# Seven block products for the four gate and up products of the second feed-forward part, in two passes of 1024 tokens

## The reference, cut to what matters

```python
Wg, Wu, Wd = dequant_nvfp4(gate...), dequant_nvfp4(up...), dequant_nvfp4(down...)
gate = jnp.einsum('th,nh->tn', xt, Wg)      # 2048 x 512 times 512 x 4096
up = jnp.einsum('th,nh->tn', xt, Wu)
gelu = jnp.tanh(0.7978845608028654 * (gate + 0.044715 * gate ** 3)) * gate * 0.5 + gate * 0.5
out = jnp.einsum('tn,hn->th', gelu * up, Wd)
...
g = _silu(out)
x = x + s * g                               # s: the recurrence over 1024 steps of each sequence
```

## Time and profile before

| | |
|---|---|
| median of 3 runs (lowest to highest) | 3084.49 us (3082.95 to 3084.57) |
| the profiled execution: its own time | 3083.76 us |
| span from first to last instruction | 3082.0 us |
| PE busy | 3028.1 us, 98% of the span |
| DVE busy | 1843.8 us, 60% |
| ACT busy | 1585.5 us, 51% |
| POOL busy | 1408.2 us, 46% |
| granted TensorE clock, mean | 0.995 |

### The profile page before, as it was taken

How to read it: one execution, slowest core, us unless ns; L and a number is a source line. 1 busy time by engine, 2 the same in 40 slices (tenths; PEclk the granted TensorE clock), 3 DMA queues, 4 the chain that set the end, 5 groups by cost and what they waited for, 6 DMA issues and landing times. The chain is left out here.

```text
span 3082.0 us, 61209 instructions
## 1 busy us (share of the span) xinstructions
PE 3028.1 (98%) x23896; PEld 2508.2 (81%) x23896; DVE 1843.8 (60%) x3306; ACT 1585.5 (51%) x3891; POOL 1408.2 (46%) x2351
## 2 busy tenths in 40 slices
PE   8999989999999999999999899999999999999999
PEld 7888867888888888888888678788888888888887
DVE  6112167788877887877888533625555555444545
ACT  5221358787788787878787633443333332112112
POOL 2322336666667666666676444323332232222212
PEclk9999999999999999999999999999999999999999
DMA  3100121111111111111111155311011110000004
GB/s 94 31 21 28 57 69 35 54 55 55 43 49 50 56 56 56 50 49 46 56 53 50 49 193 150 101 31 31 28 39 38 37 31 28 21 25 24 28 14 164
DMA packets 130240, 165.67 MB, mean 54 GB/s; under 512 B 9936, under 2 KB 72144, under 8 KB 129920
## 3 DMA queue, kind: packets, MB, share of 16 engines
q1 hardware_dynamic: 120592, 144.49, 15.6%
q10 hardware_dynamic: 9296, 17.04, 1.5%
q0 software_dynamic: 64, 0.23, 0.0%
HBM read 127.91 MB, written 33.82 MB: 52 GB/s over the span
## 5 line engine op out<-in xcount | busy, mean ns | idle before, releaser
L1489 DVE SCALAR_TENSOR_TENSOR b_zt<-b_rx,b_cw,b_zt 128x512 f32<-128x512 f32 x576 | 472.7, 821 | 22.0 <-POOL b_rx L1698 3.2
L70 PE MATMUL bank<-b_XH,b_wh 128*128 128x512 f32 x1024 | 456.5, 446 | 9.1 <-ACT b_zt L1238 7.6
L72 PE MATMUL bank<-b_XH,b_wl 128*128 128x512 f32 x1024 | 403.0, 394 | 0.0
L71 PE MATMUL bank<-b_XL,b_wh 128*128 128x512 f32 x1024 | 402.6, 393 | 0.0
L70 PE MATMUL bank<-b_XH,b_qh 128*128 128x512 f32 x1024 | 398.7, 389 | 0.0
L72 PE MATMUL bank<-b_XH,b_ql 128*128 128x512 f32 x1024 | 398.4, 389 | 0.0
L71 PE MATMUL bank<-b_XL,b_qh 128*128 128x512 f32 x1024 | 398.4, 389 | 0.0
L2758 POOL TENSOR_TENSOR b_QHL<-b_qhd,b_QHH 128x512 fp32r<-128x512 f32 x124 | 176.5, 1427 | 474.8 <-ACT b_QHH L2530 472.3
L2530 ACT CAST b_QHH<-b_qhd 128x512 fp32r<-128x512 f32 x124 | 76.8, 622 | 415.2 <-PE bank L72 254.1
L2659 DVE TENSOR_TENSOR b_QACC<-b_QACC,bank 128x512 f32<-128x512 f32 x232 | 159.0, 687 | 148.5 <-PE bank L72 148.3
L2652 DVE TENSOR_TENSOR b_qhd<-b_g,bank 128x512 f32<-128x512 f32 x128 | 87.5, 684 | 267.1 <-PE bank L72 160.9
(11 more groups left out here) (268 smaller groups left out, 7505.9 us busy)
## 6 DMA issues: line engine op xcount, KB each, us to landing
b_abc<-tmp_a SPq DMA_DIRECT2D x64, 256.0 KB, 3.4
b_gbc<-tmp_g SPq DMA_DIRECT2D x64, 256.0 KB, 3.9
tmp_og<-b_gg SPq DMA_DIRECT2D x64, 256.0 KB, 2.4
b_mo<-tmp_og SPq DMA_DIRECT2D x64, 256.0 KB, 3.2
b_wr<-in_Wk SPq DMA_DIRECT2D x16, 256.0 KB, 3.2
b_wr<-in_Wq SPq DMA_DIRECT2D x16, 256.0 KB, 4.3
b_wr<-in_Wv SPq DMA_DIRECT2D x16, 256.0 KB, 2.7
b_wr<-in_Wg SPq DMA_DIRECT2D x16, 256.0 KB, 4.2
```

The lines of the kernel that those rows point to most:

```text
L70: e.do.matmul(out, wh, xh, start=first and k == 0, stop=False)
L71: e.do.matmul(out, wh, xl, start=False, stop=False)
L72: m = e.do.matmul(out, wl, xh, start=False, stop=last and k == n - 1)
L1489: e.do.scalar_tensor_tensor(out=z[:, :], in0=rx[:, j:j + 512], scalar=cw[:, u // 2, KIND[name[0]], j:j + 1], in1=z[:, :], op0=ALU.mult, op ...
```

## The change

**Seven products.** The gate and up rows of a hidden slice (128 + 128), the two halves of the 512 inputs and two groups of 512 tokens form a 2 x 2 times 2 x 2 block product. Eight block products (6 matmuls each, 48 in all) become seven (42): m1 to m7, from the blocks a11, a12 (gate) and a22 and the sums s1 to s4 of weight blocks, and the blocks b11, b21, b22 and the sums t1 to t4 of input blocks. The weight sums are made by DVE for every block (weight_sums, 4 additions of 128 x 512). The input sums are made once for each pass.

**Two passes.** 1024 tokens a pass, 32 steps g each, 64 in all. A pass goes over all 16 blocks j, two steps for each (the hidden slices of 128). The weights are unpacked in the first pass only; each float32 tile (wG, wU, wD) is also stored to DRAM (weight_kept) and loaded again in the second pass (weight_again), where its sums, high parts and low parts are made again. Unpacking takes five integer operations for a tile rather than six.

**Sums in PSUM.** ACT copies m1 from its bank into a second one (seed); m6, m7 and m4 are added there by mm3_onto, and m2 onto m1's own bank and m3 onto m5's bank. In between ACT copies m5 and the second sum to SBUF (fifth, second_sum), DVE adds m7's state (third_sum), forms the second gate (gate1) and multiplies twice (hidden0, hidden1), ACT applies gelu twice. m4 of step g, issued in step g + 1, waits for third_sum of step g.

**Order on PE in a step:** m1; m4 and m3 of the step before; fill; m5, m6; fill; m2; fill; m7; fill. A fill is one down product (6 matmuls), and in eight of the steps also a rate product. There are three banks for the fills.

**Other.** XH1 and XL1 hold 1024 tokens; the input blocks of the second pass are kept in DRAM and swapped in during steps 31 and 32 (next_block_high, next_block_low). The first output rows are written after the first pass. All output DMAs are issued by SP.

The diff, cut to its core:

```diff
@@ in ffn1_pe @@
-        mm3(e, kb[:, :], [(t["qh"][s][:, par, q * 256 + s2 * 128:q * 256 + s2 * 128 + 128],
-                           t["ql"][s][:, par, q * 256 + s2 * 128:q * 256 + s2 * 128 + 128],
-                           XH[:, 2 * q + par, cols(n)], XL[:, 2 * q + par, cols(n)])
-                          for q in range(2) for par in range(2)]).then_inc(S["gu1"], 1)
...
+def mm3_onto(e, out, pairs):
+    for wh, wl, xh, xl in pairs:
+        e.do.matmul(out, wh, xh, start=False, stop=False, skip_group_check=True)
+        e.do.matmul(out, wh, xl, start=False, stop=False, skip_group_check=True)
+        m = e.do.matmul(out, wl, xh, start=False, stop=True, skip_group_check=True)
+    return m
...
+WEIGHTS = ("a11", "s1", "s2", "a12", "s3", "a22", "s4")
+PRODUCTS = {"m1": ("a11", "b11"), "m5": ("s1", "t1"), "m6": ("s2", "t2"), "m2": ("a12", "b21"), "m7": ("s3", "t3"),
+            "m4": ("a22", "t4"), "m3": ("s4", "b22")}
+RATE_AT = {4: 0, 10: 1, 16: 2, 22: 3, 40: 4, 46: 5, 52: 6, 58: 7}
@@ in ffn1_pe @@
+    def product(name, g):
...
+            if name == "m4":
+                e.wait_ge("c22", g + 1)
...
+        pairs = [(t["wh"][i][:, r, c], t["wl"][i][:, r, c], hi[:, r, :], lo[:, r, :]) for r in range(2)]
+        (mm3 if name in ("m1", "m5") else mm3_onto)(e, bank[to][:, :], pairs).then_inc(S[name], 1)
...
+    for g in range(2 * STEPS + 4):
+        if g <= LAST:
+            product("m1", g)
+        if 0 < g <= LAST + 1:
+            product("m4", g - 1)
+            product("m3", g - 1)
+        fill(g, 0)
+        if g <= LAST:
+            product("m5", g)
+            product("m6", g)
+        fill(g, 1)
+        if g <= LAST:
+            product("m2", g)
+        fill(g, 2)
+        if g <= LAST:
+            product("m7", g)
+        fill(g, 3)
@@ in ffn1_dve, without the swap of blocks @@
+    for g in range(2 * STEPS + 4):
+        j, odd, live, older = g // 2, g % 2 == 1, g <= LAST, 0 < g <= LAST + 1
+        sums, gate_w, up_w, down_w = odd and j + 1 < STEPS, not odd and j + 2 < 16, not odd and j + 1 < 16, odd and j < 16
+        if g:
+            fill(g - 1, 3)
+        if sums:
+            weight_sums(e, t, j + 1, 0)
+        if gate_w:
+            weight_codes(e, t, "G", j + 2, 0)
+        if older:
+            hidden0(g - 1)
+        if sums:
+            weight_sums(e, t, j + 1, 1)
+        if gate_w:
+            weight_codes(e, t, "G", j + 2, 1)
+        if older:
+            gate1(g - 1)
+        if sums:
+            weight_sums(e, t, j + 1, 2)
+        fill(g, 0)
+        if g - 3 in RATE_AT:
+            scan(RATE_AT[g - 3])
+        if older:
+            hidden1(g - 1)
+        if g - 2 in RATE_AT:
+            reset(RATE_AT[g - 2])
+            enter(RATE_AT[g - 2])
+        if gate_w:
+            weight_scaled(e, t, "G", j + 2)
+        if up_w:
+            weight_codes(e, t, "U", j + 1, 0)
+        if down_w:
+            weight_codes(e, t, "D", j, 0)
+        fill(g, 1)
...
+        fill(g, 2)
+        if up_w:
+            weight_scaled(e, t, "U", j + 1)
+        if down_w:
+            weight_scaled(e, t, "D", j)
+        if live:
+            third_sum(g)
@@ in ffn1_pool, the low parts @@
+    for g in range(2 * STEPS + 4):
...
+        if before:
+            down_low(e, t, j - 1, 0)
+        if following:
+            weight_low(e, t, 0, j + 1)
+        if older:
+            low(g - 1, 0)
+        if before and j < STEPS:
+            weight_low(e, t, 5, j)
+        if following:
+            weight_low(e, t, 1, j + 1)
+        if before and j < STEPS:
+            weight_low(e, t, 6, j)
+        if following:
+            weight_low(e, t, 2, j + 1)
+        if older:
+            low(g - 1, 1)
+        if following:
+            weight_low(e, t, 3, j + 1)
+        if before:
+            down_low(e, t, j - 1, 1)
+        if following:
+            weight_low(e, t, 4, j + 1)
```

More of the change, by code:

```diff
@@ L2099, in mix0_over @@
     e.wait_ge("mxr2", 80)
[L2104 to L2124, removed]
@@ L2127, in q_slot @@
[L2127 to L2155, removed]
@@ L2158, in down_at @@
[L2158 to L2170, removed]
-    for j in range(16):
[L2172 to L2185, removed]
@@ L2188 @@
[L2188 to L2204, removed]
+STEPS = 32
+LAST = 2 * STEPS - 1
+WEIGHTS = ("a11", "s1", "s2", "a12", "s3", "a22", "s4")
+SUMS = {"s1": 1, "s3": 2, "s2": 3, "s4": 4}
@@ L2207, in ffn1_tiles, with fill_banks, down_at @@
+def fill_banks():
+    bank, before, last, n = {}, {}, {}, 0
+    for g in range(2 * STEPS + 4):
+        for place in fills(g):
+            for what in place:
+                b = FILL_RING[n % 3]
+                bank[what], before[what] = b, last.get(b)
+                last[b] = what
+                n += 1
+    return bank, before
+FILL_BANK, FILL_BEFORE = fill_banks()
+def down_at(j, b, o):
+    return 8 * j + 4 * b + o
 def ffn1_tiles(t, at, arena):
     low = at + 32768
-    t.puts("pk", [128, 512], I32, (at, at + 2048))
@@ L2220, in ffn1_tiles @@
[L2220 to L2225, removed]
+    four = (at, at + 2048, low, low + 2048)
@@ L2489, in ffn1_pe, with fill @@
-    for j in range(1, 16):
-        for g in range(8):
-            hidden(j, g)
-            if g == DOWN_AT:
-                for i in range(len(down_order(j - 1))):
-                    down(j - 1, i)
-            if j < 9 and g < 2:
-                rate(j - 1, g)
-    for n in range(4):
-        for o in range(4):
-            down(15, 4 * n + o)
-            if n > 1 and o == 1 or n == 1 and o == 3:
-                for i in range(4):
-                    row(4 * (n - 1) + i)
-    for i in range(4):
-        row(12 + i)
+    def fill(g, place):
+        for what in fills(g)[place]:
+            if what[0] == "down":
+                down(*what[1:])
+            if what[0] == "rate":
+                rate(*what[1:])
+            if what[0] == "row":
+                row(what[1])
+            if what[0] == "sum":
+                sum_rows_pe(e, k, m, what[1], taken(what))
+            if what[0] == "turn":
+                norm_turn_pe(e, k, m, what[1], taken(what))
@@ L2627, in ffn1_act, with gate, fill @@
-    for n in range(4):
-        for o in range(4):
-            gate(n, o)
-        if n:
-            store(n - 1)
-    store(3)
+    def gate(q):
+        p, b = divmod(q, 2)
+        for o in range(4):
+            e.wait_ge("ac", down_at(16 * p + 15, b, o) + 1)
+            e.do.activation(t["QACC"][o][:, cols(b)], t["QACC"][o][:, cols(b)], ACT.Silu).then_inc(S["fsil"], 1)
+    def fill(g, place):
+        for what in fills(g)[place]:
+            if what[0] == "rate":
+                rate(*what[1:])
+            if what[0] == "sum":
+                sum_rows_act(e, k, m, what[1], bank[FILL_BANK[what]])
+                if what[1] % 2:
+                    norm_root_act(e, m, what[1] - 1)
+                    norm_root_act(e, m, what[1])
+            if what[0] == "turn":
+                norm_turn_act(e, k, m, t, what[1], bank[FILL_BANK[what]])
@@ L2654, in add, with third_sum @@
[L2654 to L2659 removed]
+    X, Y, M = t["l1x"], t["l1y"], t["l1m"]
+    def third_sum(g):
+        e.wait_ge("m7", g + 1)
+        e.wait_ge("r5c", g + 1)
+        e.do.tensor_tensor(t["c22"][:, :], t["c22"][:, :], bank[Q_BANK[g % 2]][:, :], ALU.add).then_inc(S["c22"], 1)
@@ new lines, in row, with fill @@
+        x = t["x1f"][i % 8]
+        e.do.tensor_tensor(x[:, :], bank[FILL_BANK["row", i, 0]][:, :], x[:, :], ALU.add).then_inc(S["y"], 1)
+    def fill(g, place):
+        for what in fills(g)[place]:
+            if what[0] == "down":
+                add(*what[1:])
+            if what[0] == "row":
+                row(what[1])
+            if what[0] == "sum" and what[1] % 2:
+                for i in (what[1] - 1, what[1]):
+                    norm_stats_dve(e, m, i)
+                for i in (what[1] - 1, what[1]):
+                    norm_dve(e, m, i)
```

1163 lines of the change are left out of this document (722 added, 441 removed), and 9 rows, old and new, of tables (AGAIN, SEMAPHORES).

## The result

The changed kernel takes 3168.6 us (median of 4 runs, 3165.9 to 3171.5) against 3084.5: 1.0271 times as long, 95% interval 1.0258 to 1.0284. The sign of the forecast held, its size didn't: +13 us became +84, and the time lies 29 us above the top of the range. The profiled span is 3169.8 us.

What follows compares the result with a forecast made beforehand. PE's matmul list bounded the kernel before; DVE was to bound the changed first pass. Terms -87 + 59 + 11 + 21 + 6 + 3 = +13 us gave 3098 us, range 3030 to 3140.

Steps and rivals of the forecast that it cites:

- Step 1: PE, both passes: 64 steps lose one block product of 6 matmuls each, 384 x 0.2264, -87.0 us.
- The lock and its share: First pass: POOL's SBUF operations make DVE's port work wait for 0.58 of their time, 9.7 us a pair of steps.
- Covered: Rival, first pass: waits fall into DVE's idle time, a pair stays under 30.0 us, PE sets the pace; 3012, chance 0.20.
- Step 2: Pairs 1 to 14 of the first pass: DVE needs 34.4 us against PE's 30.0, for 13.5 pairs, +59 us.
- DVE over 95%: Expected sign in first-pass windows: DVE busy over 95%, with PE at about 87%.
- the one in my rivals: Rival, first pass: late DVE delays ACT, pushing POOL's low parts into the unpacking; share 0.75, +98 us, 3137, chance 0.20.
- cover of 2.7 us: PE's one fill and m1 ahead of its wait for third_sum: 2.7 us, used up once, not in every step.
- step 3: Four recurrence slices, first pass: DVE's 4.65 us and 3.5 of waits, against 5.4 of PE's rate products, +11 us.
- Step 4: Start: DVE makes third_sum of step 0 by 1999.5 and of step 1 by 2019, later than PE needs; +21 us.
- Step 5: Step 31: DVE's 17.8 us and 5.2 of waits against 15.0, less the cover, +6 us.
- The second pass "at nothing": Second pass: DVE needs 9.9 + 2.7 of 30.0 us a pair, so PE sets the pace and nothing is added.
- Step 6: Tail: rows 8 to 11 later, last quarter's states loaded late, one queue storing all rows; +3 us (0 to 8).

Runs made afterwards that it cites:

- experiment 1: Changed kernel with POOL's low parts of weights and down weights cut to 32 of 256 columns after the first block: 3087.9 us, 1.0014 times before.
- experiment 4: Changed kernel with DVE making third_sum before the two scale multiplications of the tile in hand, same operations otherwise: 3133.7 us, 1.0160 times before.
- experiment 5: Changed kernel with POOL's two recurrence operations (`enter`) cut to 128 of 1024 columns in the first pass: 3154.2 us, 1.0229 times before.
- experiment 3: Changed kernel with 33 unused matmuls put ahead of m4 in each of the four steps with the longest stall: 3156.8 us, 1.0235 times before.
- experiment 8: Mixed kernel (eight products, then seven) with second gelu in its own step, plus up-weight low parts first and last-quarter states loaded ahead: 3083.2 us, ratio 0.9997.
- experiments 7 and 8: Mixed kernel (eight products, then seven): first, second gelu moved into its own step, 3103.5 us; then also up-weight low parts first and tail states ahead, 3083.2 us.

## Why the prediction was right in sign and wrong in size

By its own steps; the sum is set against the starts of third_sum. Forecast times add up to 3095, the span to 3169.8. (The forecast had 528 for the last two rows together; their split into 505 and 23 was made afterwards.)

| stretch | forecast | measured | miss |
|---|---|---|---|
| until third_sum of step 1 | 2019 | 2027.5 | +8.5 |
| steps 2 to 29 | 512 | 552.3 | +40.3 |
| steps 30 and 31 | 36 | 37.8 | +2 |
| steps 32 to 63 | 505 | 517.1 | +12 |
| the rest | 23 | 35.3 | +12 |

**What bounds the kernel: right.** PE's list was the time before, and a mean of 50% free engines said nothing of the first pass. PE lost 384 matmuls, and the second pass is PE's.

**Step 1, -87: right.** The count is on the page, and plain steps of the second pass take 15.0 us.

**The lock and its share: right.** DVE's timeline at the worst place, with POOL's beside it:

```profile
2357.57 0.68 DVE L3014 TENSOR_TENSOR b_QACC<-b_QACC,bank 128x512 f32<-128x512 f32 x1
2358.17 1.97 DVE L2408 TENSOR_SCALAR b_wU<-b_wU 128x512 int32<-128x512 int32 x1
2360.06 2.56 DVE L2409 TENSOR_SCALAR b_wU<-b_wU 128x512 int32<-128x512 int32 x1
2362.65 1.63 DVE L2411 TENSOR_TENSOR b_wU<-b_wU 128x512 int32<-128x512 int32 x1
```

```profile
2357.06 2.79 POOL L3138 TENSOR_TENSOR b_l1m<-b_XH,b_XL 128x1024 f32<-128x1024 f32 x1
2359.93 2.40 POOL L3140 TENSOR_TENSOR b_l1x<-b_l1x,b_l1m 128x1024 f32<-128x1024 f32 x1
2362.29 1.44 POOL L2471 TENSOR_TENSOR b_wl<-b_wG,b_wh 128x512 fp32r<-128x512 f32 x1
```

An operation of 0.42 us takes 2.56 and ends 0.29 behind POOL's; the addition from PSUM at 2357.57 lies in the midst of POOL's 2.79 and takes its usual 0.68. Over 2100 to 2500 DVE's rows are 106 us longer than the same operations undisturbed, beside 222 us of POOL's, 188 by its undisturbed durations: 0.56, where the forecast took 0.58. The exclusive lock of the Trainium skill (SBUF — State Buffer, section on the two separate sides) agrees with these rows, and experiment 1 shows what POOL's low parts cost through it. Of the rivals, Covered fell at once.

**Step 2, +59 for the first pass: the step that failed.** It said that a pair costs what DVE needs, and so counted DVE full ("DVE over 95%"). It is at 88%. In a period DVE is busy 104.9 us of 119.4, less than the 111.4 that I had added up, and idle 14.6, which stands nowhere in my sum. It is idle mostly while it waits for PE: 7.1 us for down products and 4.6 for m4 and m3. The work was sized well, even a little high; what was left out is that two engines which wait for each other in turn both have idle time.

The same period seen from PE: 95.1 us of matmuls, 16.8 of waits on third_sum, 4.9 because 24 matmuls run at the lower clock, and 2.6 of short gaps. The forecast of 111.4 leaves 16.3 for waits. So PE's waits came out almost as foretold (5.6 us a pair for 3 to 6), and the 8 us that were missing are, in PE's account, what follows the waits: every matmul had been priced at 0.2264 us. These are two accounts of one time, not two losses. The runs name its parts:

- *Order within the step.* third_sum stood behind a scaling. PE stalled for it; then DVE stood idle for m4 and m3 (1.28 and 1.27 us, until 2369.89 and 2372.45), whose operations come early in its next step. These two idle times stand behind a long stall, where six matmuls take 2.56 us rather than 1.36; with its six matmuls 0.2264 us apart m4 would have ended at about 2368.5, by my estimate from these rows, and DVE was free only at 2368.60. So these two belong as much to the clock. Changing the order alone gave back 35 us in all and 4.9 a period (experiment 4). This is a ring, but not the one in my rivals: that one raised the share of the lock to 0.75, and the share stayed where it was. It gave 3137, nearer to the time for the wrong reason.
- *Unevenness.* The recurrence's slice lies in two steps of six (25.0 and 20.9 us beside 17.6 to 19.2), and PE's rate products, which I let cover it, are issued two steps earlier, when DVE has nothing to do with them. A cover of 2.7 us carries no surplus from step to step. Cutting POOL's part of `enter` gave 3.5 a period where the lock's share alone explains 2.3 (experiment 5), so the unevenness is shown in part only. This is also what was wrong in step 3: I took 5.4 us of PE's work as cover, and it was spent elsewhere. (Its 3.37 for the scan was too high on the other side; see the last section.)
- *The clock.* Stalls of 9.7 us are followed by thirteen matmuls at half rate; filling the four longest gave 12 us in all, 3.3 a period (experiment 3). In PE's account of steps 2 to 29 the matmuls at half rate cost 22 us, where 40 were missed. The forecast had no price for what follows a wait.

4.9 + 3.5 + 3.3 are 11.7 where 8.0 were missing, so they cannot simply be added. That each of the three gives time back is shown one at a time; how they share the 40 us is not. A shorter stall did not always mean less time at the lower clock: in experiment 4 the matmuls at half rate rose from 108 to 131.

**Step 4, start: +21 was +30.** third_sum of step 0 came at 2007.0 for 1999.5, the next 20.5 us later, as forecast (19.5).

**Step 5: right** within 2 us.

**The second pass "at nothing": 12 us short.** Waits of 5.7 (step 32, on third_sum of step 31) and 4.6 (ACT's second_sum, four times 1.1, in the steps with rate products and their table loads).

**Step 6, tail: +3 was about +15.** The mechanism was named, the states of the last quarter loaded only when the third is used up, but not priced as a chain. The end of the chain of the kernel after shows it:

```profile
3151.28 1.30 DVE b_QACC L3035 x2
...
3153.90 5.30 DMA b_s1f<-tmp_s
3159.33 1.77 POOL b_QACC L3163
3161.11 1.68 POOLq L3208
3162.88 3.66 PE bank L2783 x16
```

Load, product, and transposes at half rate (3.66 us for the 16, against 1.97 from the first start to the last end in the kernel before; the granted clock from 3160 to 3167 is 0.50). Loading into another tile went with half of the wait (6.8 to 3.2 us, experiment 8).

**The range.** Its top was the ring's time with nothing above it. Idle time and matmuls at the lower clock add to every case with DVE as the bound, and the range had no term for either.

## What to carry to other kernels

When two engines take turns within a step, neither need be full: sum their work, then add the time in which each waits for the other and the slower matmuls behind PE's waits, and put the operation that the other engine needs ahead of everything that can wait. Before packing an engine's work into half the time, ask what the other engine on its port does then; here 81 us hung on POOL's low parts, with DVE's list unchanged. An arithmetic saving on the engine that bounds the kernel belongs where the others have slack: seven products in the second pass alone, with eight in the first, took 46 us off, and with the repairs of experiments 7 and 8 brought 3168.6 down to 3083.2, and so only level with before. No run tried seven products in both passes with the order of experiment 4 and the other repairs together.

## What the runs showed of the hardware that was not expected

Two groups of the kernel after, duration in ns as min/median/max (the first from 2100 to 2500):

```profile
L2409 DVE TENSOR_SCALAR b_wU<-b_wU x10: 411/1521/2558, 2121.4 to 2479.5; 128x512 int32<-128x512 int32 x10
```

```profile
L3028 DVE TENSOR_TENSOR_SCAN b_l1x<-b_l1y,b_l1x x8: 2283/2671/3061, 2135.9 to 3097.9; 128x1024 f32<-128x1024 f32 x8
```

- A tensor_scalar with one SBUF input waits for POOL as fully as one with two: 0.41 us became 1.52 as a median and 2.56 at most. At 2360.06 it had started only 0.13 us behind POOL's operation, and waited for nearly all of that one's 2.40.
- The scan of 1024 elements took 2.28 to 3.06 us in the kernel after, where all eight took 3.36 to 3.38 before, with the same form of instruction. The traces show what decides: where an operation of POOL started ahead of the scan, the scan ends 2.15 to 2.2 us behind the end of that one. Before, POOL's started 0.08 ahead of the scan and lasts 1.29; in the second pass of the kernel after 0.38 ahead, and the scan takes 3.06 (first two lines below). In the first pass POOL's next operation starts 1.5 behind the scan, which then takes 2.28, and POOL's takes 1.85 instead of 1.29. In experiment 1 POOL's is cut to 0.32 and all eight scans take 2.28 (last two lines). So the undisturbed scan takes 2.28 us, and the 3.37 of the forecast's step 3 held 1.1 of waiting for POOL.

```profile
2802.89 1.29 POOL L2471 TENSOR_TENSOR b_wl<-b_wS,b_wh 128x512 fp32r<-128x512 f32 x1 [0.70 <-ACT b_wh L2465]
2803.27 3.06 DVE L3028 TENSOR_TENSOR_SCAN b_l1x<-b_l1y,b_l1x 128x1024 f32<-128x1024 f32 x1
...
2724.68 0.32 POOL L2472 TENSOR_TENSOR b_wl<-b_wS,b_wh 128x64 fp32r<-128x64 f32 x1 [0.84 <-ACT b_wh L2465]
2724.91 2.28 DVE L3030 TENSOR_TENSOR_SCAN b_l1x<-b_l1y,b_l1x 128x1024 f32<-128x1024 f32 x1
```

- PE's idle time has a price beyond itself: 33 superfluous matmuls in each of four stalls made the kernel 12 us faster.
